# A deformable-attention stage on one core: half takes between tiles, split output products, a third down buffer, idle TensorE products

## The reference, cut to what matters

```python
x = x + autocorrelation_attention(layernorm(x), ctx)   # L0_xattn
x = x + frequency_ffn(layernorm(x))                    # L0_ffn
x = x + deformable_attention(layernorm(x), ctx)        # L1_xattn
x = x + quantised_ffn(layernorm(x))                    # L1_ffn, 4-bit weights, 16-bit activations
```

```python
v    = (ctx @ w_value + b_value)                      # 16 heads of 16
off  = (xn @ w_off + b_off).reshape(B, L, H, 4, 2)    # 4 points a head
attw = softmax((xn @ w_attw + b_attw).reshape(B, L, H, 4))
ix   = ((clip(off[..., 0], 0, 1) + 1) * L - 1) / 2    # a position between L/2 - 0.5 and L - 0.5
sampled = v[floor(ix)] * (1 - fx) * hy + v[floor(ix) + 1] * fx * hy
out  = einsum('bhlpd,bhlp->blhd', sampled, attw) @ w_out + b_out
```

## Time and profile before

| what | value |
|---|---|
| runs | 1018.9, 1020.79, 1007.04 us; median 1018.9 |
| the profiled execution | 1004.41 us, its span 1002.6 us |
| mean granted TensorE clock | 0.932 |
| busy: PE, DVE, ACT, POOL | 838.5, 684.9, 539.4, 306.0 us |
| first `up_sides` of sampling, last output product | 410.5 us, 637 us |

### The profile page before, as it was taken

How to read it: one execution, slowest core, us unless ns; L and a number is a source line. 1 busy time by engine, 2 the same in 40 slices (tenths; PEclk the granted TensorE clock), 3 DMA queues, 4 the chain that set the end, 5 groups by cost and what they waited for, 6 DMA issues and landing times.

```text
span 1002.6 us, 12939 instructions
## 1 busy us (share of the span) xinstructions
PE 838.5 (84%) x4501; PEld 539.6 (54%) x4501; DVE 684.9 (68%) x1237; ACT 539.4 (54%) x1009; POOL 306.0 (31%) x236
## 2 busy tenths in 40 slices
PE   4999998799999998788888899599998994005998
PEld 3776675577777886244444444344443441004887
DVE  2567767866775676579888888735534999895333
ACT  2444434455334665666666666134428995982432
POOL 2100000566110222587777778200010431000000
PEclk9999999799999999599999999799998997556999
DMA  9800000010000000000000000000002436710111
GB/s 290 256 1 1 1 1 1 0 55 0 2 11 1 1 1 1 0 2 1 1 1 1 2 1 2 1 0 1 0 1 84 168 146 275 262 71 11 53 52 53
DMA packets 23446, 45.41 MB, mean 45 GB/s; under 512 B 2323, under 2 KB 18646, under 8 KB 22230
## 3 DMA queue, kind: packets, MB, share of 16 engines
q1 hardware_dynamic: 21776, 43.08, 12.1%
q10 hardware_dynamic: 1606, 1.52, 0.5%
HBM read 27.80 MB, written 16.78 MB: 44 GB/s over the span
## 4 chain that ended last, share of the span: by engine, by line
PE 60%; DVE 20%; POOL 8%; ACT 6%; issue 5%; ACTq 1%; DMA 0%; DVEq 0%; POOLq 0%
PE pair L1313 8%; PE pair L1272 8%; POOL hat L596 5%; PE pair L967 5%; PE pair L1194 4%; PE pair L1075 3%; PE pair L1102 3%; PE pair L1208 3%; PE pair L971 3%; DVE peak L1758 2%; DVE wide L1753 2%; DVE peak L1743 2%; DVE wide L1781 2%; PE pair L1012 2%; PE pair L1104 2%
## 5 line engine op out<-in xcount | busy, mean ns | idle before, releaser
L596 POOL TENSOR_TENSOR hat<-hat 128x1024 f32<-128x1024 f32 x62 | 145.6, 2360 | 45.1 <-DVE hat L1619 44.4
L1178 PE MATMUL pair<-rows,sel 32*128 32x512 bf16 x256 | 75.4, 397 | 23.1 <-ACT down_b L816 17.3
L1619 DVE SCALAR_TENSOR_TENSOR hat<-pair,down_a 128x1024 f32<-128x1024 f32 x64 | 78.1, 1220 | 21.8 <-PE pair L1170 19.7
L1297 PE MATMUL pair<-xqs,wuT 128*128 128x512 f32 x192 | 85.9, 610 | 4.8 <-ACT up_stage L861 4.8
L816 ACT ACTIVATE down_b<-pair 128x512 f32<-128x512 f32 x128 | 69.4, 595 | 37.0 <-PE pair L1178 32.1
L816 ACT ACTIVATE down_a<-pair 128x512 f32<-128x512 f32 x128 | 69.5, 595 | 33.5 <-PE pair L1178 24.0
L1313 PE MATMUL pair<-wdT,hid 128*128 128x256 f32 x384 | 84.8, 384 | 2.9 <-DVE hid L1800 2.9
L1619 DVE SCALAR_TENSOR_TENSOR hat<-pair,down_b 128x1024 f32<-128x1024 f32 x64 | 78.0, 1219 | 11.9 <-PE pair L1170 11.7
L1272 PE MATMUL pair<-xqs,wgT 128*128 128x512 f32 x192 | 85.1, 601 | 0.0
L1313 PEld LDWEIGHTS pair<-wdT,hid 128*128 128x128 f32 x384 | 74.1, 193 | 13.5 <-DVE hid L1800 3.2
L513 POOL TENSOR_TENSOR rstd<-lnt,half 128x8 f32<-128x8 f32 (+2 forms) x15 | 26.5, 1769 | 167.5 <-DVE lnt L1354 167.5
(11 more groups left out here) (208 smaller groups left out, 1880.8 us busy)
## 6 DMA issues: line engine op xcount, KB each, us to landing
up_far<-up_stage SPq DMA_DIRECT2D x24, 512.0 KB, 2.6
ups<-up_far SPq DMA_DIRECT2D x8, 1536.0 KB, 6.7
x_sb<-in_x_dram SPq DMA_DIRECT2D x8, 512.0 KB, 8.2
c_sb<-in_ctx_dram SPq DMA_DIRECT2D x8, 512.0 KB, 9.0
out_dram<-x_sb SPq DMA_DIRECT2D x16, 256.0 KB, 2.1
four<-in_c_four_dram SPq DMA_DIRECT2D x1, 1280.0 KB, 5.7
deq<-in_L_ffn_w_gate_dram SPq DMA_DIRECT2D x1, 768.0 KB, 6.8
deq<-in_L_ffn_w_up_dram SPq DMA_DIRECT2D x1, 768.0 KB, 8.5
```

The source lines that it names most:

```text
L596: nc.gpsimd.tensor_tensor(hat[:, n % RING, :], hat[:, (n - 2) % RING, :], hat[:, n % RING, :], ALU.add).then_inc(summed, 1)
L1178: mm(bank[6 + i], sel[g:g + 32, pp, 1, :], rows[g:g + 32, q, c * 2 + a, :], start=True, stop=True).then_inc(down_mm, 1)
L1297: last = mm(bank[2 + oc], wuT[:, c, oc * 128:(oc + 1) * 128], xqs[:, t % 2, c, :], start=(c == 0), stop=(c == DC - 1))
L1619: V.scalar_tensor_tensor(hat[:, n % RING, :], pair[n % 2][:].rearrange("p i t -> p (i t)"), 0.0, down[n % 2][:].rearrange("p i t -> p (i t ...
```

## The change

1. A third `down` buffer; a relu waits for the hat of tile n-3.
2. `take` is cut in halves: the first two sequences of sum k after the second down product of an odd tile (`between`, place 2), the other two after `up_sides` of the even tile that follows (place 0).
3. `project_att` in four parts of one product (two instructions) each, `clear_att` in halves of 256 columns, put between single down products; there are three places in a tile.
4. Idle products (`keep_busy`, bf16, 512 columns, K = 128, results unused): one at each place of tiles 0 to 12 of the first quad, 6 + 10 around `turn_w63`, 6 ahead of sampling, 36 after it; and `keep_rest`: 16 fp32 products of 512 columns ahead of `spread_peak(4)`, once `o_done` is 14.
5. In the offset stage ACT does `exponent` first in a tick, `keep_v63(0)` and `(1)` come two ticks later and behind the parts, and TensorE does `turn_parts` ahead of `values63`, and `turn_w63` ahead of it.
6. DVE: the second `add_out` at tick 10, not 11, and an extreme at 11, not 10.

```diff
-down = [down_a, down_b]
+down = [down_a, down_b, sb("down_c", [128, 2, QUAD * L], F32, sample)]
...
+        for tick, step in ((2, exponent), (10, keep_rows), (7, second_part), (5, first_part)):
+            if group_at(t, tick) is not None:
+                step(group_at(t, tick))
+        if t == S5 + B + 3:
             keep_v63(0)
             keep_v63(1)
-        for tick, step in ((10, keep_rows), (7, second_part), (2, exponent), (5, first_part)):
-            if group_at(t, tick) is not None:
-                step(group_at(t, tick))
         if t == S5 + B + 5:
             keep_v63(2)
             keep_v63(3)
...
     def sample_act(n):
         for i in range(2):
             act.wait_ge(down_mm, 2 * n + i + 1)
-            if n >= 2:
-                act.wait_ge(hat_done, n - 1)
-            nc.scalar.activation(down[n % 2][:, i, :], bank[6 + i], ACT.Relu).then_inc(down_done, 1)
+            if n >= 3:
+                act.wait_ge(hat_done, n - 2)
+            nc.scalar.activation(down[n % 3][:, i, :], bank[6 + i], ACT.Relu).then_inc(down_done, 1)
...
+    def keep_busy(n, place):
+        for _ in range(n):
+            mm(place, idn16[:], rows[:, 0, 0, :], start=True, stop=True)
...
             turn_gw(GW_TICKS.index(t))
         nth(t, S5, turn3)
         nth(t, S5 + 1, project3)
+        if t == S5 + B + 6:
+            pe.wait_ge(v_kept, B)
+            pe.wait_ge(off_kept, B)
+            keep_busy(6, bank[3])
+            turn_w63()
+            keep_busy(10, bank[3])
+        if group_at(t, 9) is not None:
+            turn_parts(group_at(t, 9))
         if t == S5 + B + 1:
             for p in range(NQ // 2):
                 values63(p)
-        if t == S5 + B + 6:
-            turn_w63()
-        if group_at(t, 9) is not None:
-            turn_parts(group_at(t, 9))
+    keep_busy(6, bank[3])
...
-    def down_sides(n):
+    def down_side(n, i):
+        q, c, r, pp, a, m, g = tile_of(n, i)
+        if n:
+            pe.wait_ge(down_done, 2 * n + i - 1)
+        mm(bank[6 + i], sel[g:g + 32, pp, 1, :], rows[g:g + 32, q, c * 2 + a, :], start=True, stop=True).then_inc(down_mm, 1)
+    def take_from(tile, b, stop):
         for i in range(2):
+            q, c, r, pp, a, m, g = tile_of(tile, i)
+            h = c * 128 + 32 * m
+            last = mm(bank[4 + c][32 * m:32 * m + 32, b * 128:(b + 1) * 128], vz[:, r, b, h:h + 32],
+                      hat[:, tile % RING, i * QUAD * L + b * 128:i * QUAD * L + (b + 1) * 128],
+                      start=False, stop=stop, skip_group_check=True)
+        return last
+    def take_half(k, half):
+        if half == 0:
+            if k % 4 == 0:
+                pe.wait_ge(vz_ready, k // 2 + 2)
+            pe.wait_ge(summed, k + 1)
+        for b in (2 * half, 2 * half + 1):
+            last = take_from(last_of_sum(k), b, k % 4 >= 2 and b == QUAD - 1)
+        if half:
+            last.then_inc(taken, 1)
+    def take_both(k):
         n = last_of_sum(k)
+        for tile in (n - 2, n):
+            pe.wait_ge(hat_done, tile + 1)
             for b in range(QUAD):
+                last = take_from(tile, b, k % 4 >= 2 and tile == n and b == QUAD - 1)
         last.then_inc(taken, 1)
+    def project_att(q, i, part):
+        if part == 0:
+            pe.wait_ge(attT_copied, 2 * q + 2)
+            if i:
+                pe.wait_ge(x3_done, 2 * q + 1)
+            mm(bank[5][:].rearrange("p (b d) -> p b d", b=2), ones3,
+               bias3[:, BAT["bout"]:BAT["bout"] + D].unsqueeze(1).broadcast_to([3, 2, D]), start=True, stop=False)
+        b, c = part // DC, part % DC
+        last = mm(bank[5][:, b * D:(b + 1) * D], attT[:, c, (2 * i + b) * L:(2 * i + b + 1) * L], wout_sb[:, c, :],
+                  start=False, stop=(part == 2 * DC - 1))
+        if part == 2 * DC - 1:
+            last.then_inc(out_mm, 1)
+    def clear_att(q, c, half):
+        if half == 0:
+            if c == 0:
+                pe.wait_ge(edge_ready, 2 * q + 2)
+            if q:
+                pe.wait_ge(attT_copied, 2 * (q - 1) + c + 1)
+                if c == 1:
+                    pe.wait_ge(x3_done, 2 * q)
+        last = mm(bank[4 + c][:, half * 256:(half + 1) * 256], v63m[:, c * 128:(c + 1) * 128],
+                  w63m[:].rearrange("p b t -> p (b t)")[:, half * 256:(half + 1) * 256],
+                  start=(half == 0), stop=True, skip_group_check=True)
+        if half:
+            last.then_inc(edge_used, 1)
+    def between(n, place):
+        q, t = n // TURN, n % TURN
+        if place == 0 and n >= 6 and n % 2 == 0:
+            take_half((n - 6) // 2, 1)
+        if place == 2 and n >= 5 and n % 2 == 1:
+            take_half((n - 5) // 2, 0)
+        for tick, c in ((4, 0), (12, 1)):
+            for half in range(2):
+                if (t, place) == (tick + c, 1 + half - c):
+                    clear_att(q, c, half)
         if q:
+            for i, spots in enumerate((((6, 1), (6, 2), (7, 0), (7, 1)), ((9, 1), (10, 1), (10, 2), (11, 0)))):
+                if (t, place) in spots:
+                    project_att(q - 1, i, spots.index((t, place)))
+        elif t < 13:
+            keep_busy(1, bank[5])
     def sample_pe(n):
-        q, t = n // TURN, n % TURN
         up_sides(n)
-        if n + 1 < PAIRS:
-            down_sides(n + 1)
-        if t in (4, 13):
-            clear_att(q, t // 8)
-        if n >= 5 and n % 2 == 1:
-            take((n - 5) // 2)
-        if q and t in (6, 10):
-            project_att(q - 1, t // 10)
+        for place in range(3):
+            between(n, place)
+            if n + 1 < PAIRS and place < 2:
+                down_side(n + 1, place)
-    down_sides(0)
+    down_side(0, 0)
+    down_side(0, 1)
     for n in range(PAIRS):
         sample_pe(n)
-    take(SUMS - 2)
-    take(SUMS - 1)
-    project_att(NQ - 1, 0)
-    project_att(NQ - 1, 1)
+    take_half(SUMS - 3, 1)
+    take_both(SUMS - 2)
+    take_both(SUMS - 1)
+    for i in range(2):
+        for part in range(2 * DC):
+            project_att(NQ - 1, i, part)
+    pe.wait_ge(hat_done, PAIRS)
+    keep_busy(36, bank[3])
...
+    def keep_rest():
+        for _ in range(16):
+            mm(bank[3], wdT[:, 0, 0:128], wdT[:].rearrange("p c o -> p (c o)")[:, 0:512], start=True, stop=True)
...
     pe.wait_ge(up_kept, UPS)
+    pe.wait_ge(o_done, HALVES - 2)
+    keep_rest()
     spread_peak(4)
     staggered(pe, B, [(0, down_product)])
...
         if n >= RING:
             dve.wait_ge(taken if n % 4 >= 2 else summed, (n - RING) // 4 * 2 + n % 2 + 1)
         V.scalar_tensor_tensor(hat[:, n % RING, :], pair[n % 2][:].rearrange("p i t -> p (i t)"), 0.0,
-                               down[n % 2][:].rearrange("p i t -> p (i t)"), ALU.max, ALU.min).then_inc(hat_done, 1)
+                               down[n % 3][:].rearrange("p i t -> p (i t)"), ALU.max, ALU.min).then_inc(hat_done, 1)
         q, t = n // TURN, n % TURN
-        if q and t in (7, 11):
-            add_out(q - 1, t // 11)
+        if q and t in (7, 10):
+            add_out(q - 1, t // 10)
         if q and t in (8, 12):
             two_moments(q - 1, t // 12)
-        if q and t in (9, 10):
-            two_ends(q - 1, 0, t - 9)
+        if q and t in (9, 11):
+            two_ends(q - 1, 0, t // 11)
         if q and t in (13, 15):
             two_ends(q - 1, 1, t // 15)
```

More of the change, by code:

```diff
@@ L799, in _ @@
                 nth(t, S5 + 1, keep_v)
-                if t == S5 + B + 1:
+                for tick, step in ((2, exponent), (10, keep_rows), (7, second_part), (5, first_part)):
+                    if group_at(t, tick) is not None:
+                        step(group_at(t, tick))
+                if t == S5 + B + 3:
                     keep_v63(0)
                     keep_v63(1)
-                for tick, step in ((10, keep_rows), (7, second_part), (2, exponent), (5, first_part)):
-                    if group_at(t, tick) is not None:
-                        step(group_at(t, tick))
                 if t == S5 + B + 5:
@@ L1171, in up_sides @@
                 last.then_inc(up_mm, 1)
-            def down_sides(n):
-                for i in range(2):
[L1175 to L1183, removed]
-                n = last_of_sum(k)
[L1185 to L1189, removed]
-                    for b in range(QUAD):
[L1191 to L1196, removed]
-                last.then_inc(taken, 1)
@@ L1200, in project_att @@
[L1200 to L1208, removed]
-                                  start=False, stop=(b == 1 and c == DC - 1))
-                last.then_inc(out_mm, 1)
@@ L1212, in clear_att @@
-            def clear_att(q, c):
-                if c == 0:
-                    pe.wait_ge(edge_ready, 2 * q + 2)
-                if q:
-                    pe.wait_ge(attT_copied, 2 * (q - 1) + c + 1)
-                    if c == 1:
-                        pe.wait_ge(x3_done, 2 * q)
-                mm(bank[4 + c], v63m[:, c * 128:(c + 1) * 128], w63m[:].rearrange("p b t -> p (b t)"),
```

(3 more changed lines are left out.)

## The result

The changed kernel takes 1047.3 us (median of 1046.94, 1046.58 and 1047.57), the kernel before 1013.0 (median of four, 1006.3 to 1020.8) on the same chip: ratio 1.033, 95% interval 1.022 to 1.045. The forecast was 1032, range 1006 to 1050: the direction of the sum was right and its size about half of what came.

A forecast was written before the change was run, and what follows sets the result against it. A sampling loop through TensorE and ACT, not DVE, was taken as the bound. Terms -4.6, +5.9, +15.7, +1.9, 0 and +3.3 sum to +22.2 on 1004.4, 1026.6; with 5 added, 1032, range 1006 to 1050.

The forecast's parts named there:

- The ring: Sampling loop of down products, relus, next second down product, take: 2.92 us a pair, sets the 27.3 us quad.
- Rival 1: In sampling, DVE's wait for `up_sides` is the bound: quad falls to 24.4, time 985 to 990; chance 7%.
- The half takes: In sampling, half takes around `up_sides` lengthen a pair by 0.32 to 3.24 us, +2.6 for eight pairs.
- The tail: End of the offset stage, reordered: sampling starts about 4.6 us earlier, -4.6 (-3 to -6).
- the third buffer: Third down buffer in sampling: worth 0, it only hides DVE's lateness from ACT.
- the 36: 36 idle products after sampling: +1.6 before `spread_peak(0)`, -2.0 in the gate, taken as 0 (-0.5 to +1.6).
- `keep_rest`: Idle products before the down stage: delay `spread_peak(4)` by 5.0, give back 1.7 by the clock; +3.3 (+1.7 to +6.7).
- rival 3: The clock isn't held; idle products at half clock in first quad, `keep_rest` and before `spread_peak(0)`: 1043; chance 17%.
- each part costs its 0.48 and a start of 0.32 ... Gain 0: Split output products and clears in a sampling quad cost +4.0 together, as whole ones did, so gain 0.
- the first quad, +5.9: 39 idle products lengthen the first sampling quad to 39.2 from 33.3 us, full clock repaying only a part: +5.9.
- the 5 us added for the spread of before: 5 of the 14.5 us between profiled execution and median of the runs before, added to 1026.6: 1032.
- Rival 2: Starts cost nothing: half takes 0, first quad +2.4, last quad 0.3; 1005.8, with the 5 us 1011; chance 17%.

The follow-up runs named there:

- late halves: Kernel before, second half take ahead of even tiles' down products, first half behind: 1.008; with new offset tail, third buffer, idle products 0.997; GpSimd copies moved too, 0.988.
- the last kernel: Kernel before with new offset tail, third down buffer, first-quad idle products, moved GpSimd copies and whole takes behind the odd tile's down products: 1022.1 us, ratio 1.017.

## Why the prediction was right in part

**Right.** The ring through TensorE and ACT is the loop of a free pair, not DVE's wait of the earlier trace rows. Rival 1 (halves shorten the quad to 24.4) is refuted by a quad of 32.07 and by half takes alone; a wait that is half a microsecond long in a list is not yet in the loop. The half takes were put at +2.6 a quad; with whole takes and products in parts the quad is 29.51, with half takes 32.07, +2.56; with whole products 27.3 and 29.65, +2.35 (30.0 in half takes alone, +2.7). That this fits is partly luck: a free pair grew by 0.40 where 0.32 was put, and eight times 0.40 would be 3.2. The tail (-5.4 without the later start, range -3 to -6), the third buffer (0), the 36 (+0.3 for 0) and `keep_rest` (+3.2 for +3.3) stand. The rule of the Trainium skill that the prediction cites ("TensorE: Matmul & The Clock Gate", Part 3, "The mechanism") goes with 0.32 between each 32-row product and the half take after it, never 0.21. It does not go with the inside of a half take, where eight loads on all 128 rows stand among eight products that follow each other at 0.055, the time of their 128 columns; there the measurement decides.

**Right by luck: the range.** 1047.3 lies in 1006 to 1050 only because rival 3, the lost clock, set the upper end. The forecast by itself was put at 1020 to 1044, and "over 2% slower", which came, was given 0.30. The changed kernel lost no time to the clock; it was longer by the terms below.

**Overlooked: GpSimd was already on the chain.** The prediction takes 27.3 as explained by the ring of TensorE and ACT, and has GpSimd only as "a short wait" in the clear at tick 4. The chain of the kernel before runs once in each quad from a hat through three of GpSimd's sums and the copies between them to a take:

```profile
517.40 1.24 DVE hat L1619
518.71 2.37 POOL hat L596
...
525.75 2.33 POOL hat L596
528.08 0.14 issue
528.21 1.07 PE pair L1194 x16
```

That is 9.4 us of GpSimd's work, and the take waited 0.36 for it. So a shorter TensorE ring could gain 0.36 us in that stretch before GpSimd held it. GpSimd's share of the whole chain is 8% in the kernel before and 1% in the changed one, whose TensorE work is longer.

**Wrong: "each part costs its 0.48 and a start of 0.32 ... Gain 0."** This is the step that carried most of the error. Between whole and split the quads differ by 29.51 - 27.3 = 2.2 with whole takes and 32.07 - 29.65 = 2.4 with half takes. Six quads of it are 13 us of the 20.3 that the sum was short. A part holds TensorE 0.64, not 0.48, since the end of a group is paid once a group: 8 x 0.16 for the parts, 4 x 0.10 for the halves of clears (0.63 for 0.53) and 8 x 0.08 for the free pairs make 2.3, and the quad missed by 32.07 - 29.9 = 2.2. The same term is in the free pair, 3.32 for my 3.24: 0.56 for a half take where I had halved 1.00. Dividing a group's length was the mistake, and the trace of before could have shown it: 24 gate products of 512 columns in a row take 10.30, 0.43 each, and a clear of two such takes 1.05 and not 0.86, so 0.19 is its end.

**Wrong: the first quad, +5.9 for a measured +11.2.** I gave each idle product one start, ahead of it. The trace has another one behind it, 0.32 from product to product:

```profile
412.32 0.39 PE L1181 MATMUL pair<-rows,sel 32*128 32x512 bf16 x2
412.64 0.39 PE L1136 MATMUL pair<-rows,idn 128*128 128x512 bf16 x1
412.96 0.39 PE L1189 MATMUL pair<-rows,sel 32*128 32x512 bf16 x1
...
414.24 0.39 PE L1181 MATMUL pair<-rows,sel 32*128 32x512 bf16 x2
```

A tile without a take takes 414.24 - 412.32 = 1.92, six steps of 0.32, where I had 1.62; a pair with a take 4.96, where I had 4.24.

**Wrong, and it helped: the 5 us added for the spread of before.** The changed kernel's profiled execution is the median of its compared runs, which lie within 1 us, so nothing had to be added. Without it the forecast would have been 1027; the 5 covered a quarter of the missing 20.

**Not foreseen: what the clock hangs on.** Rival 3 had the clock lost in spite of the idle products; in the traced execution it held, so rival 3 is not what made the 1047. But I had weighed the first quad's idle products only against 11.5 us at half clock. They decide the whole stage: without them 1192.3. None of my cases had a price like it.

Rival 2 (starts cost nothing, 1011) is refuted by every 0.32 above.

The moments named for the check came: the first `up_sides` at 406.35, full clock from 395 on, ACT idle 1.16 a pair, `spread_peak(4)` 5.2 late. The quads of 29.9 did not.

**Still open.** Why the clock holds in one order of the same products and falls in another. In the traces of steady sampling it holds in the kernel before, the changed one with half or whole takes, and those with late halves; it falls with halves and whole products, and with whole takes in the last kernel. Each of these edits changes TensorE's waits together with the order of its products, so which of the two decides isn't settled. Nor were the first quad's idle products of the changed kernel cut down by steps; in the order with late halves 16 in the first quad sufficed (1.00 from 380 to 635).

## What to carry to other kernels

Cost a group of matmuls as a start, so many columns, and an end, and never by a mean per instruction: where an fp32 group is split so that other products fit between, each cut costs one start and one end, here some 0.3 us (0.10 and 0.2), and it pays only where the engine would wait that long. First close the ring (down product, relus, the product that needs the bank, the take) to the measured period, then read the chain for a second path that is nearly as long, before looking for work that can leave the ring; half takes inside the ring lost 2.4 us a quad, and half takes behind D gained 1.0, but only after GpSimd's copies had been moved (27.8 and 27.25 before that). And when a product sequence is reordered, look at the granted clock before anything else: by my count three of twelve kernels here (no idle products in the first quad, half takes alone, the last one) lost more by the clock than by all of their instructions.

## What the runs showed that I had not expected

Without the first quad's idle products the granted clock fell from 2.4 to 1.2 GHz while TensorE did nothing but 32-row products, and stayed there for the rest of the sampling stage, 145 us in all; with 39 products on all 128 rows of 0.32 us each in the first quad the traced execution stayed at 2.4, also in the quads behind it that have none. And GpSimd, 21.8 us busy in a quad of 27.3, already held a take back by 0.36 once a quad in the kernel before, and held the quad at 27.25 when TensorE's list was rearranged; moving its copies into its idle time gave 0.64 a quad.
